# Delta rule on one Trainium2 core: decay products of levels 0 to 4 in one step for all eight chunks

## What is computed

```python
q = l2norm(silu(conv(x @ Wq))) * 128 ** -0.5
k = l2norm(silu(conv(x @ Wk)))
v = silu(conv(x @ Wv))
g = exp(-softplus(x @ Wfa @ Wfb + dt_bias) * exp(A_log))     # decay, one per token and key feature
beta = sigmoid(x @ Wb)
def step(S, inp):                                            # scan over the 1024 tokens
    qt, kt, vt, gt, bt = inp
    S = S * gt[..., None]
    delta = (vt - kt @ S) * bt[..., None]
    S = S + kt[..., None] * delta[:, :, None, :]
    return S, qt @ S
o = rmsnorm(o) * norm_w * sigmoid(x @ Wga @ Wgb)
x = x + o.reshape(B, T, 16 * 128) @ Wo
```

## Time and profile before

| | us |
|---|---|
| median of 3 runs | 1602.77 (1600.35 to 1605.79) |
| the profiled execution, by the clock outside | 1604.8 |
| its span, first to last instruction | 1603.0 |
| delta rule, steady part, one head (mean of 15 distances) | 56.4 |

### The profile page before, as it was taken

The page is one execution under the profiler, slowest core; times in us unless marked ns, Lnnn a source line. Parts: engine busy times, 40 slices in busy tenths (PEclk is TensorE's granted clock), DMA queues, the critical chain, the costliest instruction groups (busy, mean ns, idle before and its releaser), DMA issues. The chain is left out here.

```text
span 1603.0 us, 41748 instructions
## 1 busy us (share of the span) xinstructions
PE 1402.7 (88%) x15104; PEld 931.1 (58%) x15104; DVE 1199.3 (75%) x3775; ACT 1019.8 (64%) x2716; POOL 41.2 (3%) x49
## 2 busy tenths in 40 slices
PE   6897889979899878888989989988989989978788
PEld 2544556665456346656756766665666667566634
DVE  6867888966822497888888888898988988984221
ACT  5627978985610565877767787686787777754220
POOL 0000000000000000000000000000000000000000
PEclk9999999989999999999999999999999999979999
DMA  4034000000030011121211212212121221200010
GB/s 169 0 100 114 13 21 22 2 2 0 1 135 0 28 40 43 18 66 52 70 20 57 65 20 64 60 23 60 58 63 19 68 55 25 51 26 15 0 56 26
DMA packets 128489, 69.30 MB, mean 43 GB/s; under 512 B 104464, under 2 KB 115984, under 8 KB 127264
## 3 DMA queue, kind: packets, MB, share of 16 engines
q1 hardware_dynamic: 128288, 66.64, 15.5%
HBM read 51.36 MB, written 6.98 MB: 36 GB/s over the span
## 5 line engine op out<-in xcount | busy, mean ns | idle before, releaser
L1675 DVE SCALAR_TENSOR_TENSOR arena<-arena 128x1024 f32<-128x1024 f32 x144 | 183.1, 1281 | 19.6 <-ACT arena L1245 19.3
L892 PE MATMUL bank<-xt,arena 128*128 128x512 f32 x384 | 184.0, 611 | 9.3 <-ACT arena L1237 7.7
L1754 DVE TENSOR_TENSOR arena<-arena 128x512 f32<-128x512 f32 x224 | 155.4, 694 | 7.4 <-PE bank L948 2.7
L720 PE MATMUL bank<-xt,arena 128*128 128x512 f32 x320 | 141.5, 598 | 3.8 <-DVE arena L1488 3.8
L1244 ACT COPY arena<-bank 128x512 f32<-128x512 f32 x96 | 56.2, 586 | 93.8 <-PE bank L892 92.3
L892 PEld LDWEIGHTS bank<-xt,arena 128*128 128x128 f32 x384 | 69.0, 196 | 72.1 <-issue 71.9
L720 PEld LDWEIGHTS bank<-xt,arena 128*128 128x128 f32 x320 | 60.0, 191 | 84.8 <-issue 84.6
L948 PEld LDWEIGHTS bank<-arena 128*32 128x32 f32 x5120 | 58.7, 113 | 77.1 <-issue 66.0
L739 PE MATMUL bank<-arena 128*128 128x256 f32 (+2 forms) x384 | 95.6, 395 | 6.2 <-DVE arena L1488 5.3
L1174 ACT ACTIVATE arena<-arena 128x128 f32<-128x128 f32 x256 | 99.6, 393 | 0.0
L948 PE MATMUL bank<-arena 128*32 128x32 f32 x5120 | 73.9, 202 | 27.1 <-DVE arena L1756 18.2
(11 more groups left out here) (170 smaller groups left out, 3307.3 us busy)
## 6 DMA issues: line engine op xcount, KB each, us to landing
arena<-d_w SPq DMA_DIRECT2D x16, 519.0 KB, 6.6
arena<-beta_scratch SPq DMA_DIRECT2D x16, 512.0 KB, 6.0
arena<-zero_scratch SPq DMA_DIRECT2D x14, 512.0 KB, 4.8
arena<-arena SPq DMA_DIRECT2D x64, 64.0 KB, 2.5
arena<-zero_scratch SPq DMA_DIRECT2D x15, 256.0 KB, 2.9
arena<-arena SPq DMA_DIRECT2D x12, 256.0 KB, 3.8
arena<-w_scratch SPq DMA_DIRECT2D x2, 1376.0 KB, 6.2
arena<-f_idx SPq DMA_DIRECT2D x2, 1072.0 KB, 8.4
```

Of the source, the lines that this page charges most:

```text
L720: last = pe.matmul(bank[2 * w + n % 2][0:rows, :], (WU if f < 2 else WU1R)[:, w, k, m * P:m * P + rows], XT[:, k, hf * HALF:(hf + 1) * HAL ...
L892: last = pe.matmul(bank[b][:], DW[:, par, c:c + P], XT[:, k, rhs], start=(k == 0), stop=(k == KC - 1))
L1675: dve.scalar_tensor_tensor(out=CT[:, x], in0=RAW[:, x, 3 - j:3 - j + S], scalar=DW[:, par, tap:tap + 1], in1=CT[:, x], op0=ALU.mult, op1=A ...
L1754: dve.tensor_tensor(kq, kq, left, ALU.mult)
```

## The change

Levels 0 to 4 and the advances behind them take all eight chunks in one step (`gr` is then `BOTH`). The steps alternate between banks 2 and 3 by the level's parity. The masked copy writes 128 x 256 in place of twice 128 x 128, the advance has one product of 128 x 1024 and one of 128 x 512 in place of two of 128 x 512 and two of 128 x 256, and level 3 and level 4 have one tick each. PE's matmuls are the same ones, 32 in a row. Levels 5 and 6 stay as they are. The tables of `PLACE` have new places for all steps. Core of the diff:

```diff
+BOTH = 2
 PLACE = {
     "pe": [
-        (1.267, "level", 0, 1), (1.281, "level", 0, 0), (1.322, "turn_v", 1), (1.363, "level", 1, 1), (1.39, "level", 1, 0),
+        (1.287, "level", 0, 2), (1.331, "turn_v", 1), (1.375, "level", 1, 2), (1.449, "level", 2, 2), (1.493, "level", 3, 2),
...
 def banks_of(step):
+    if what == "level" and step[2] == BOTH:
+        return (2 + step[1] % 2,)
...
                 def blocks(m, par):
-                    sp.wait_ge(blocks_ready, 2 * m + 2)
+                    sp.wait_ge(blocks_ready, m + 1)
...
             def dr_level(n, par, lv, gr):          # PE
-                b = 2 + gr
+                b = banks_of(("level", lv, gr))[0]
-                    pe.wait_ge(kq_step, done("dve", n, "advance", lv - 1, gr))
-                for t in range(4):
-                    c = 4 * gr + t
-                    if lv < STRIP_LEVELS:
+                    pe.wait_ge(kq_step, done("dve", n, "advance", lv - 1, gr if lv > STRIP_LEVELS else BOTH))
+                if gr == BOTH:
+                    for c in range(NT):
                         for k in range(P // STRIP):
...
             def dr_level(n, par, lv, gr):          # DVE
-                out = MBC[:, par, 4 * gr:4 * gr + 4].rearrange("p c w (b r s) -> p (c w) b r s", r=2, s=s)[:, :, :, 1, :]
-                mask = MKC[:, lv, :].rearrange("p (a b s) -> p a b s", a=1, s=s).broadcast_to([P, 8, BLK // s, s])
+                out = MBC[:, par].rearrange("p c w (b r s) -> p (c w) b r s", r=2, s=s)[:, :, :, 1, :]
+                mask = MKC[:, lv, :].rearrange("p (a b s) -> p a b s", a=1, s=s).broadcast_to([P, 2 * NT, BLK // s, s])
...
             def dr_advance(n, par, lv, gr):        # DVE
-                cs = slice(gr * HALF, (gr + 1) * HALF)
-                nb = HALF // s
+                cs = slice(0, S) if gr == BOTH else slice(gr * HALF, (gr + 1) * HALF)
+                nb = (cs.stop - cs.start) // s
```

More of the change, by code:

```diff
@@ new lines @@
+        (2.184, "left", 5, 0), (2.272, "left", 6, 0), (2.289, "keys", 0), (2.325, "left", 6, 1), (2.342, "right", 6, 0),
+        (2.395, "solve", 0), (2.412, "keys", 1), (2.447, "right", 6, 1), (2.465, "update", 0), (2.535, "solve", 1),
+        (2.57, "update", 1), (2.605, "solve", 2), (2.658, "update", 2), (2.728, "solve", 3), (2.746, "update", 3),
+        (2.816, "solve", 4), (2.851, "update", 4), (2.904, "solve", 5), (2.956, "update", 5), (3.009, "solve", 6),
+        (3.061, "update", 6), (3.149, "solve", 7), (3.202, "update", 7), (3.237, "final"), (3.36, "rows", 0),
@@ L93 @@
+        (3.482, "rows", 1),
     ],
     "dve": [
[L95 to L98 removed]
```

111 lines of the change are left out of this document (53 added, 58 removed).

## The result

| | us |
|---|---|
| median of the kernel after, 4 runs | 1650.95 (1644.68 to 1656.91) |
| median of the kernel before, 4 runs beside it | 1604.28 (1600.35 to 1606.63) |
| ratio, with its 95% interval | 1.0276 (1.0240 to 1.0312) |
| span of the profiled execution, before and after | 1603.0 and 1655.1 |
| mean granted clock, before and after | 0.971 and 0.953 |

The forecast was 1595.7, and its range ended at 1608. The 3.6 us more per head are the whole loss: 15 x 3.6 = 54 against 52 of the spans.

What follows compares the result with a forecast made beforehand. A chain across engines bound each head, through XX's DMAs in even heads and PE in odd ones. Even heads 0, seven odd heads x 0.8 = 5.6, ends 1.5: 7.1 off the median 1602.77 gives 1595.7, range 1584 to 1608.

Steps and rivals of the forecast that it cites:

- The levels: Levels 0 to 3 on PE and DVE: the tick of level 3 comes 0.8 us earlier per head.
- The sum: Whole kernel: even heads 0, seven odd heads x 0.8 = 5.6, ends 1.5; 7.1 us less in all.
- the forecast 2.5: DVE waits for PE: some 1 us ahead of each of advances 1 and 2, 0.5 ahead of level 3.
- From the tick to `less`: DVE: 7.3 us to `invert`, 1.2 earlier, cancelled by the third tap's 1.19; `less` begins where it did.
- "Everything from there to XX is as before": Even heads: from `less` through the DMAs into XX nothing changes, so nothing is gained at `left 4 0`.
- PE, from 0.8 less in odd heads: PE from `less` to `left 4 0` in odd heads: 0.8 us less, between 0 and the spare 1.6.
- the 0.39 I had counted: PE's wait for DVE ahead of solve 4, 0.39 us, is filled by `project 0`.
- the other half of advance 4, 0.93: DVE between the level-3 tick and `invert`: merging level 4 adds 0.93 us there.
- Rival D: PE's instruction-supply stalls at level 3: four more cost 8 us, 1604; none, 1590. Over 1607.5 with C: 0.17.
- C: Tick less than 0.8 early, third tap ahead of `less`: XX 0.8 later in even heads, +6, about 1608; 0.17 with D.

Runs made afterwards that it cites:

- run 5 against 1: Kernel after with DVE's norm_q read moved ahead of the first tap (1: 1640.3 us); run 5 also moves ACT's flip ahead of update 3: 1627.5 us.
- run 10: Run 8's kernel with DVE's update 2 moved two steps of less sooner: 1603.4 us, ratio 0.9977.
- run 11: Run 10's kernel with level 4 in two halves again, levels 0 to 3 still merged: 1594.0 us, ratio 0.9917.
- runs 11 and 12: Level 4 in two halves again: run 11 as above; 12 in the kernel after with nothing else changed, 1639.1 us, ratio 1.0219.
- run 8: Kernel after with norm_q read, flip and third tap moved (1620.9 us), plus SP's bulk loads issued behind the decay blocks: 1605.5 us.

## Why the prediction was wrong

*The levels: right where nothing disturbed them, wrong in the mean.* DVE's busy time fell by 15.8 us, and the merge is worth 16 us in the new order. In undisturbed heads (13.5 to 13.9 behind `key 2`, before 14.1 to 14.4) the tick came some 0.5 to 0.9 earlier where 0.8 was forecast. In the mean of heads 1 to 14 it came 0.6 later: the stops of PE all lie ahead of a tick, eight in after and four in before, and stretches at half grant fell into other heads. The sum had no term for either. DVE's waits ahead of advances 1 and 2 and of level 3 were 0.36, 1.41 and 0.59 in the mean, in sum near the forecast 2.5.

*From the tick to `less`: wrong, and this is the first step of the sum that failed with no disturbance to blame.* I summed DVE's own instructions, 7.3, and took it that nothing else would stop it. I had compared the orders of DVE for this stretch, but not PE's with the banks in mind. `piece 0` behind `norm_q` makes PE wait 1.75 for DVE, DVE then 0.65 for PE, and `invert` came at 8.13. The tap behind it was rightly priced at 1.19, and I let it cancel a gain that was not there. `less` came 9.67 behind the tick, where the sum gave 8.9 (7.3 + 0.45 + 1.19), and 10.16 in the mean of heads 1 to 14 against 8.72 in before.

*"Everything from there to XX is as before": wrong.* ACT's flip had moved behind `update 3`, 0.87 per head in the mean of the trace, 13 us in run 5 against 1. The sentence was about three engines and I had looked at one.

*PE, from 0.8 less in odd heads: wrong.* Odd heads got 3.8 us longer, even ones 3.7. Some waits of PE did shrink, that for DVE ahead of the solves (L1041, now L1042) from 14.6 to 4.9 us between 700 and 1400, which is more than the 0.39 I had counted. New ones outweighed them: 21.0 us at the piece and 11.3 at predict 3 in the same twelve heads, against none and 2.7. Of these the one at the piece cost time and the one at predict 3 did not (run 10).

*Level 4: priced right and put on the wrong side.* The sum had the other half of advance 4, 0.93, ahead of `invert`; run 11 gives 0.83 in head 7 and 0.59 in the mean, and runs 11 and 12 a price of 9 and 12 us. I let the earlier tick pay for it, and did not see that level 4 is the one level whose second half nothing ahead of XX needs soon, so that the change could have left it out.

*Rival D: came true, and its price was too low.* Four stops more were its case, and eight against four there are, with 7.9 us more; I had priced them at 8, so 1604. (I had them all at level 3, where the four of before are; of the eight, five are at level 2, two at level 3 and one in a piece.) But without them after is 21 us faster and before 6, which leaves 15 for the difference. A part of what is over may be the lower clock, though the grant fell within 3 us behind two of the eight stops only. The Trainium skill ("Runtime: NRT & Kernel Launch", section on instruction fetch) says that this fetch is mostly hidden; 15 us for four moved DMAs (run 8) speak against it for a PE with 64 short matmuls in a row beside DMA shares of 0.86 to 0.95.

*The clock: missing from the sum.* No term of it and no rival priced what an idle us of PE does to the matmuls behind it. 22.7 of the 52.1 us between the profiled executions are that, and by the estimate above some 10 of the 47 between the medians.

*Direction.* The rival that ended slower, C, was the right kind (the chain to XX gets longer, 0.75 per head), at 0.17 with D. Its condition, a tick less than 0.8 early, held in the mean, but by D's stops and the clock and not by PE waiting for whole advances (0.2 us between 700 and 1400), and XX came 3.1 later where it had 0.8. What was left out was that several such things come together in a table where every row was renumbered, and that they add.

What stays open: kernel 11 is 6 us faster than kernel 7 (before with the bulk loads moved), about what the merge of levels 0 to 3 might give, but the two differ in many rows and I didn't part them. No kernel has levels 0 to 3 alone merged in the order of before. And why the loads bring on the stops isn't shown, only that the stops go with them.

## What to carry to other kernels

When steps are merged, ask of each whether anything waits for its first half alone: levels 0 to 3 brought their tick 0.7 forward where nothing disturbed them, and level 4, whose second half could stand behind `less`, lost 9 to 12 us. When an order is written anew, compare it engine by engine for every pair of steps that share a buffer or stand in one chain (here bank 0, the flip and the tap), since two rows that changed places (`norm_q` and the flip, 24 us) cost more than the 22 instructions saved per head brought (16 us). Compare over all heads, not in the one that looks cleanest. And try large loads where the matmul queue is made of few long instructions, not of many short ones: here that gave 6 to 21 us.

## What the hardware showed that I had not expected

- A stop of PE of 2 us can cost more than 2 us: behind an idle time of 2.30 the grant stayed at half for some 17 us with PE busy throughout, and 200 matmuls took 17.5 us in place of 12.0. In the whole kernel a mean grant of 0.953 in place of 0.971 made the same matmuls 22.7 us longer. Three stops of 2.05 to 2.11 us had nothing of the kind behind them.
- Four DMAs of 1.8 MB together (256, 512, 512 and 519 KB), moved by some 17 us within a head, took PE's stops inside the short matmuls from 8.1 to 1.0 us in 700 us, and by a move of 15 us the kernel before gained 6 us. At each of the twelve stops a 16 KB packet of instructions lands 1.2 to 1.6 us before PE goes on.
- A wait of 0.8 us in each head, plain in the trace of the engine that is busiest, was worth no more than the spread (run 10), and the second half of level 4 on DVE ahead of `invert`, which shows as no wait at all, was worth 9 to 12 us.
